# Moving layer-norm pieces and the order of GpSimd's work in a fused attention and FFN kernel

## The chip, the cores and the metric

The kernel runs on one core of one Trainium2 chip. The metric is the device time of one execution in microseconds (us). TensorE (PE in the profile) multiplies matrices, VectorE (DVE), ScalarE (ACT) and GpSimd (POOL) work on 128 partitions at once, and SyncE (SP) issues most of the DMA transfers. Each engine runs its own list of instructions in order and waits on semaphores for the others.

## What is computed

x has the shape 8 x 1024 x 128 (batch, position, channel). With H = 8 heads:

```python
def layer(x, proj_q, proj_k, proj_v, proj_o, w1, w2):
    xn = (x - mean(x)) / sqrt(var(x) + 1e-5)              # over the 128 channels
    Q = einsum('bnd,hdk->bhnk', xn, proj_q)
    K = einsum('bmd,dk->bmk', xn, proj_k)                 # one key head, one value head
    V = einsum('bmd,dv->bmv', xn, proj_v)
    weights = softmax(einsum('bhnk,bmk->bhnm', Q, K))
    O = einsum('bhnm,bmv->bhnv', weights, V)
    Y = einsum('bhnv,hdv->bnd', O, proj_o)
    mid = einsum('amh,ehn->aemn', xn, w1)                 # linear, 8 experts summed
    return x + Y + einsum('aemn,enh->amh', mid, w2)
```

## The kernel before

The weights are folded once at the start: query and key projections into one matrix per head (a_hi, a_lo), value and output projections into another (c_hi, c_lo), and the two FFN weights into a single 128 x 128 matrix (f_hi, f_lo). Every large product is done in float16 with operands split into a high half and a low half; the product of the two low halves is left out.

The 8192 positions are 64 tiles of 128. Work is cut into 64 pairs (batch, head), each of two blocks of 512 queries, each block of four units of 128 queries against all 1024 keys: 512 units, one for each period of the main loop. All engines count the same periods n, and nine more empty the pipeline. A pair is 8 periods; "period 3" below means n = 3 modulo 8.

In a period TensorE computes the high part of the scores of unit n (L499), turns the row of maxima of unit n-1 (L527), does one to three tiles of the products of weights with values of an older block (weigh, L398 to L400 on t_ps), some small products (small_products: the projection of the next block, head_out on s_ps, the FFN of one tile, the transposition of a normalised tile), then the low parts of the scores of unit n-1 (low_passes, L512 and L514), and at the end it transposes the key maxima of unit n (L523). The low passes of unit n-1 wait for the bias, which VectorE copies into a row of g_lo (place_bias, L742).

VectorE in period n: place_bias(n-1), the maximum over keys of unit n (max_of_keys, L729), then between_maxima(n) (scaling of head outputs L752/L756 and FFN outputs L764, the copy of a turned tile L769, the low half of the projection L725 or of the values t_lo L746), then find_max(n) (L734), then before_bias(n). In periods 3 and 7 (row_later) the maximum over keys is ahead of place_bias, and TensorE does both halves of the high pass in one piece. Tiles from number 10 (AHEAD) on are normalised one per pair, in before_bias: bn_stats (L805) in period 2, bn_aggr (L647) in period 3, plus EPS (L811) in period 6, and in the next pair the scaling `normalise` (L650) in period 2 and the cast to float16 `split_high` (L657) in period 3. GpSimd takes the power -1/2 (L317) in period 7 and the low half xn_low (L273) in period 4 of the next pair. Tile 10 + p belongs to pair p, so pairs 0 to 53 have one.

ScalarE: the exponentials of unit n-1 (L357), their high half p_high (L364), g_high (L351) in periods 1 and 5, t_high (L370) in periods 2 and 6. p_high is not done in periods 1 and 5 and twice in periods 2 and 6.

GpSimd: the low half p_low of unit n-1 (L281), the addition of head outputs to xacc (add_head, L293) and of FFN outputs (add_ffn, L299). Within a period the additions and the normalisation pieces stand ahead of p_low. weigh waits for all four low halves of its block.

exponentials(u) waits for p_low of unit u-4, since there are PR = 4 buffers of exponentials; scale_head(k, g) waits for the addition of block k-1 with the same g, since y_tmp has one buffer for each g.

## Time and profile before

| quantity | value |
| --- | --- |
| time, median of 3 runs | 1693.48 us (1692.24 to 1694.28) |
| time of the profiled execution | 1692.57 us |
| its span, first to last instruction | 1690.8 us |
| mean granted TensorE clock | 0.999 |
| busy: TensorE | 1655.1 us, 98% |
| busy: GpSimd | 1335.8 us, 79% |
| busy: ScalarE | 1294.1 us, 77% |
| busy: VectorE | 1281.2 us, 76% |
| weight loads | 1212.9 us, 72% |

The busy time of TensorE is modelled from starts, so 98% does not mean that it is at its peak; a short gap shows in the distance between the starts of two products, not always in the idle column. The granted clock is 1.00 at 2.4 GHz and 0.50 at 1.2 GHz.

### The profile page before, as it was taken

What the parts mean: (1) busy time and instruction counts of PE and PEld (TensorE: products, weight loads), DVE (VectorE), ACT (ScalarE), POOL (GpSimd) and SP (SyncE); (2) the same over time, 40 slices, a digit from 0 to 9 for tenths busy, and PEclk for the clock granted to TensorE, in tenths of its full rate; (3) what the DMA queues carried; (4) which work ended last, traced back from release to release, by engine and by line L of the source; (5) the groups of instructions that cost most, each with busy time, mean ns of one, the idle gap of its engine ahead of it and who ended that gap; (6) DMA issues with size and microseconds to landing.
All of it is one profiled execution on the core that took longest, in us unless ns stands there. A gap on an engine that the chain in (4) does not pass through costs nothing. (4 is left out here: it accounts for less than half of the span.)

```text
span 1690.8 us, 46211 instructions
## 1 busy us (share of the span) xinstructions
PE 1655.1 (98%) x18820; PEld 1212.9 (72%) x18820; DVE 1281.2 (76%) x2761; ACT 1294.1 (77%) x1296; POOL 1335.8 (79%) x956
## 2 busy tenths in 40 slices
PE   7999999999999999999999999999999999999997
PEld 6777777777777777777777777777777777777774
DVE  5777777777777777777777777777777777777774
ACT  4777777777777777777777777777777777877874
POOL 2687888788788788878878878887887888788785
PEclk9999999999999999999999999999999999999999
DMA  7000000000000000000000000000000000000000
GB/s 227 2 2 2 2 2 14 2 2 2 8 8 2 1 2 8 8 2 2 2 8 8 2 1 2 8 8 2 2 2 14 2 2 2 2 14 2 2 2 13
DMA packets 16175, 16.71 MB, mean 10 GB/s; under 512 B 416, under 2 KB 12192, under 8 KB 15968
## 3 DMA queue, kind: packets, MB, share of 16 engines
q1 hardware_dynamic: 14928, 13.24, 2.7%
q8 instruction: 152, 2.49, 0.6%
q10 hardware_dynamic: 1040, 0.52, 0.1%
q14 instruction: 55, 0.45, 0.1%
HBM read 9.57 MB, written 4.19 MB: 8 GB/s over the span
## 5 line engine op out<-in xcount | busy, mean ns | idle before, releaser
L281 POOL TENSOR_TENSOR pr_lo<-pr,pr_hi 128x1024 f16<-128x1024 f32 x512 | 1087.7, 2135 | 328.5 <-ACT pr_hi L364 328.5
L357 ACT ACTIVATE pr<-s_ps,boost,scale 128x1024 f32<-128x1024 f32 x512 | 616.9, 1205 | 241.3 <-PE s_ps L514 222.4
L729 DVE TENSOR_REDUCE key_max<-s_ps 128x128 f16<-128x1024 f32 x512 | 625.7, 1222 | 0.1
L364 ACT ACTIVATE pr_hi<-pr 128x1024 f16<-128x1024 f32 x512 | 525.4, 1051 | 8.1
L512 PE MATMUL s_ps<-g_lo,xT 128*128 128x128 f16 x4096 | 512.9, 219 | 2.1 <-DVE g_lo L742 1.0
L514 PE MATMUL s_ps<-g_hi,xT 128*128 128x128 f16 x4096 | 512.3, 219 | 0.0
L512 PEld LDWEIGHTS s_ps<-g_lo,xT 128*128 128x128 f16 x4096 | 399.3, 98 | 41.7 <-DVE g_lo L742 11.1
L514 PEld LDWEIGHTS s_ps<-g_hi,xT 128*128 128x128 f16 x4096 | 400.8, 98 | 29.9
L398 PE MATMUL t_ps<-pr_hi,xn_hi 128*128 128x512 f16 x1024 | 388.3, 379 | 16.9 <-POOL pr_lo L281 3.2
L400 PE MATMUL t_ps<-pr_hi,xn_lo 128*128 128x512 f16 x1024 | 388.4, 379 | 0.0
L399 PE MATMUL t_ps<-pr_lo,xn_hi 128*128 128x512 f16 x1024 | 388.4, 379 | 0.0
L499 PEld LDWEIGHTS s_ps<-g_hi,xT 128*128 128x128 f16 x4096 | 282.3, 98 | 91.7 <-ACT g_hi L351 1.4
L499 PE MATMUL s_ps<-g_hi,xT 128*128 128x128 f16 x4096 | 333.6, 219 | 1.9 <-ACT g_hi L351 1.2
L742 DVE CAST g_lo<-turn_ps 1x128 f16<-1x128 f32 x512 | 141.4, 276 | 177.0 <-PE turn_ps L527 172.4
L293 POOL TENSOR_TENSOR xacc<-xacc,y_tmp 128x256 f32<-128x256 f32 x256 | 186.6, 729 | 9.3 <-DVE y_tmp L756 9.1
L400 PEld LDWEIGHTS t_ps<-pr_hi,xn_lo 128*128 128x128 f16 x1024 | 100.0, 98 | 121.3 <-issue 0.6
L734 DVE TENSOR_REDUCE minus_max<-turn_ps 128x1 f16<-128x128 f16 x512 | 147.8, 289 | 39.2 <-PE turn_ps L523 38.9
L725 DVE TENSOR_TENSOR g_lo<-s_ps,g_hi 128x512 f16<-128x512 f32 x127 | 87.8, 691 | 90.0 <-ACT g_hi L351 90.0
L370 ACT ACTIVATE t_hi<-t_ps 128x512 f16<-128x512 f32 x128 | 76.4, 597 | 92.5 <-PE t_ps L400 92.5
L756 DVE SCALAR_TENSOR_TENSOR y_tmp<-s_ps,scale,recip 128x256 f32<-128x256 f32 x256 | 123.6, 483 | 26.9 <-DVE recip L752 0.5
L398 PEld LDWEIGHTS t_ps<-pr_hi,xn_hi 128*128 128x128 f16 x1024 | 99.9, 98 | 52.0 <-issue 31.9
L523 PE MATMUL turn_ps<-ident,key_max 128*128 128x128 f16 x512 | 112.1, 219 | 0.1
(117 smaller groups left out, 1548.0 us busy)
## 6 DMA issues: line engine op xcount, KB each, us to landing
out_dram<-xacc SPq DMA_DIRECT2D x16, 256.0 KB, 2.3
w_sb<-in_L_ffn_w_dram SPq DMA_DIRECT2D x1, 2048.0 KB, 10.0
pr<-in_L_attn_proj_q_dram ACTq DMA_DIRECT2D x1, 512.0 KB, 4.4
xacc<-in_L_attn_x_dram SPq DMA_DIRECT2D x2, 256.0 KB, 4.9
pr<-in_L_attn_proj_o_dram SPq DMA_DIRECT2D x1, 512.0 KB, 6.3
xacc<-in_L_attn_x_dram SPq DMA_DIRECT2D x1, 128.0 KB, 6.2
wkv<-in_L_attn_proj_k_dram SPq DMA_DIRECT2D x1, 64.0 KB, 2.7
wkv<-in_L_attn_proj_v_dram SPq DMA_DIRECT2D x1, 64.0 KB, 4.2
```

The lines of the kernel that those rows point to most:

```text
L281: pool.tensor_tensor(pr_lo[:, u % RING, :], pr32[:, u % PR, :], pr_hi[:, u % RING, :], ALU.subtract)\
L293: pool.tensor_tensor(acc, acc, y_tmp[:, g, :, :], ALU.add).then_inc(y_added, 1)
L357: act.activation(pr32[:, u % PR, :], both_banks(u), ACT.Exp, bias=boost[:, 0:1], scale=scale[:, 0:1])\
L364: act.activation(pr_hi[:, u % RING, :], pr32[:, u % PR, :], ACT.Copy).then_inc(p_hi_ready, 1)
L398: pe.matmul(dst, lhs_hi, rhs_hi, start=start, stop=False)
L399: pe.matmul(dst, lhs_hi, rhs_lo, start=False, stop=False)
L400: return pe.matmul(dst, lhs_lo, rhs_hi, start=False, stop=stop)
L499: last = pe.matmul(dst[:, i * P:(i + 1) * P], x_hi(keys + i), g_hi[:, k % 2, j * P:(j + 1) * P], start=i == 0, stop=False, skip_group_chec ...
L512: pe.matmul(dst, x_hi(batch_tile(k) + t), g_lo[:, k % 2, j * P:(j + 1) * P], start=False, stop=False, skip_group_check=True)
L514: last = pe.matmul(dst, x_lo(batch_tile(k) + t), g_hi[:, k % 2, j * P:(j + 1) * P], start=False, stop=True, skip_group_check=True)
L729: dve.tensor_reduce(key_max[:, u % 2, :], both_banks(u).rearrange("p (t q) -> p q t", q=P), AX_X, ALU.max).then_inc(keys_max, 1)
L734: dve.tensor_reduce(minus_max[:, u % 2, 0:1], turn16[:, 0:P], AX_X, ALU.max, negate=True)\
```

## The change

Seven edits. (1) In GpSimd's loop p_low(n-1) comes first in the period; the head additions that were in periods 3 modulo 4 and 0 modulo 4 come one period later, behind p_low. (2) VectorE's bn_stats, bn_aggr and plus EPS go from periods 2, 3 and 6 to 0, 1 and 4; the power goes from period 7 to 3. (3) The scaling `normalise` of tiles 10 and later goes from VectorE to GpSimd, in period 6 of the same pair (normalise_next). (4) Their cast split_high goes from VectorE to ScalarE, in period 0 of the next pair, behind p_high. (5) xn_low goes from period 4 to period 2 of the next pair. (6) In periods 0 and 4 TensorE does the FFN product and the transposition ahead of head_out(k-3, 1), and VectorE empties them in the same order. (7) The DMA of tiles 10 to 63 becomes two, of tiles 10 to 15 ahead of w2 and of 16 to 63 behind it. bn_aggr gets a wait for the scaling of the tile before (ln_xn32), since GpSimd reads the single slot of mean and variance.

```diff
--- before.py
+++ after.py
@@ -115,7 +115,7 @@
         turn16 = turn_ps[:, :].bitcast(F16)
 
         q_in, o_in, kv_in = sem("q_in"), sem("o_in"), sem("kv_in")
-        x_in = [sem("x_in%d" % n) for n in range(4)]
+        x_in = [sem("x_in%d" % n) for n in range(5)]
         w1_in, w2_in = sem("w1_in"), sem("w2_in")
         consts, slot_set = sem("consts"), sem("slot_set")
         transposed, evacuated, kv_ready, folded, c_copied = (
@@ -234,8 +234,9 @@
             sp.dma_start(wo_sb, wo.rearrange("h d v -> d h v")).then_inc(o_in, 16)
             sp.dma_start(xacc[:, NT:AHEAD, :], x_tiles[:, NT:AHEAD, :]).then_inc(x_in[2], 16)
             sp.dma_start(w1_sb[:, :, :], w1.rearrange("e h n -> h e n")).then_inc(w1_in, 16)
+            sp.dma_start(xacc[:, AHEAD:2 * NT, :], x_tiles[:, AHEAD:2 * NT, :]).then_inc(x_in[3], 16)
             sp.dma_start(w2_sb[:, :, :, :], w2.rearrange("e (c p) d -> p e c d", p=P)).then_inc(w2_in, 16)
-            sp.dma_start(xacc[:, AHEAD:TILES, :], x_tiles[:, AHEAD:TILES, :]).then_inc(x_in[3], 16)
+            sp.dma_start(xacc[:, 2 * NT:TILES, :], x_tiles[:, 2 * NT:TILES, :]).then_inc(x_in[4], 16)
 
             for b in range(B):
                 for half in range(2):
@@ -275,6 +276,14 @@
 
             xn_low(HT, HT, HT)
 
+            def normalise_next(tile):
+                pool.wait_ge(ln_rstd, tile + 1)
+
+                pool.wait_ge(ln_hi, tile)
+                pool.wait_ge(xn_ready, tile)
+                pool.tensor_scalar(xn32[:, 0, 1:D], xacc[:, tile, 1:D], mean_var[:, AHEAD, 0:1],
+                                   rstd[:, AHEAD:AHEAD + 1], ALU.subtract, ALU.mult).then_inc(ln_xn32, 1)
+
             def p_low(u):
 
                 pool.wait_ge(p_hi_ready, u + 1)
@@ -303,30 +312,36 @@
                 k, at = divmod(n, 4)
                 if n == 2:
                     xn_low(NT, NT, AHEAD - NT)
-                if at == 3 and 0 <= k - 2 < BLOCKS:
-                    add_head(k - 2, 0, ffn_adds)
-                    head_adds += 1
+                if 1 <= n <= UNITS:
+                    p_low(n - 1)
                 if at == 0 and 0 <= k - 3 < BLOCKS:
-                    add_head(k - 3, 1, ffn_adds)
+                    add_head(k - 3, 0, ffn_adds)
                     head_adds += 1
                 if (tile := ffn_tile(n)) is not None:
                     add_ffn(tile, head_adds)
                     ffn_adds += 1
-                if n % 8 == 7 and (tile := ln_tile(n // 8)) is not None:
+                if at == 1 and 0 <= k - 3 < BLOCKS:
+                    add_head(k - 3, 1, ffn_adds)
+                    head_adds += 1
+                if n % 8 == 3 and (tile := ln_tile(n // 8)) is not None:
                     pool.wait_ge(ln_var, tile - AHEAD + len(FIRST_TILES) + 1)
                     pool.tensor_tensor(rstd[:, AHEAD:AHEAD + 1], var_eps[:, AHEAD:AHEAD + 1],
                                        minus_half[:, 0:1], ALU.pow).then_inc(ln_rstd, 1)
-                if n % 8 == 4 and (tile := ln_tile(n // 8 - 1)) is not None:
+                if n % 8 == 6 and (tile := ln_tile(n // 8)) is not None:
+                    normalise_next(tile)
+                if n % 8 == 2 and (tile := ln_tile(n // 8 - 1)) is not None:
                     xn_low(tile, 0, 1)
-                if 1 <= n <= UNITS:
-                    p_low(n - 1)
 
         @block.scalar
         def _(act):
             act.dma_start(wq_sb, wq.rearrange("h d k -> d h k")).then_inc(q_in, 16)
-            def split_high(tile):
-                act.wait_ge(ln_xn32, tile + HT)
-                act.activation(xn_hi[:, tile:tile + HT, 1:D], xn32[:, tile:tile + HT, 1:D], ACT.Copy).then_inc(ln_hi, HT)
+            def split_high(tile, row, tiles):
+                act.wait_ge(ln_xn32, tile + tiles)
+                if tile > NT:
+                    act.wait_ge(ln_hi, tile)
+                at = tile % KEEP
+                act.activation(xn_hi[:, at:at + tiles, 1:D], xn32[:, row:row + tiles, 1:D], ACT.Copy)\
+                   .then_inc(ln_hi, tiles)
 
             def empty_w1(e):
                 act.wait_ge(w1_turned, e + 1)
@@ -334,10 +349,10 @@
 
             act.wait_ge(transposed, 2)
             act.activation(wqT, s_ps[:, 0:N].rearrange("p (h k) -> p h k", h=H), ACT.Copy).then_inc(evacuated, 1)
-            split_high(0)
+            split_high(0, 0, HT)
             act.wait_ge(transposed, 3)
             act.activation(woT, s_ps[:, N:2 * N], ACT.Copy).then_inc(evacuated, 1)
-            split_high(HT)
+            split_high(HT, HT, HT)
             act.wait_ge(folded, 2)
             act.activation(c32[:, :], s_ps[:, N:2 * N], ACT.Copy).then_inc(c_copied, 1)
             act.wait_ge(scales, 1)
@@ -387,6 +402,8 @@
                     p_high(n - 2)
                 if at != 1 and 1 <= n <= UNITS:
                     p_high(n - 1)
+                if n % 8 == 0 and (tile := ln_tile(n // 8 - 1)) is not None:
+                    split_high(tile, 0, 1)
                 if n == 7:
                     act.wait_ge(scales, 2)
                     act.activation(c_hi[:, :, 0:P], c32[:, :].rearrange("p (h k) -> p h k", h=H), ACT.Copy,
@@ -592,8 +609,6 @@
                     if k >= 3:
                         pe.wait_ge(y_scaled, 2 * (k - 2))
                     head_out(k - 2, 0)
-                if at == 0 and 0 <= k - 3 < BLOCKS:
-                    head_out(k - 3, 1)
                 if (tile := ffn_tile(n)) is not None:
                     pe.wait_ge(weights_ready, 4)
                     three_pass(ffn_part(n), x_hi(tile), x_lo(tile), f_hi[:, :], f_lo[:, :]).then_inc(ffn_ps, 1)
@@ -601,6 +616,8 @@
                     pe.wait_ge(xn_ready, tile + 1)
                     pe.transpose(turned_part(n)[:, 0:P], xn_hi[:, tile % KEEP, :], ident16[:, :])
                     pe.transpose(turned_part(n)[:, P:2 * P], xn_lo[:, tile % KEEP, :], ident16[:, :]).then_inc(xT_ps, 1)
+                if at == 0 and 0 <= k - 3 < BLOCKS:
+                    head_out(k - 3, 1)
 
             row_of_amax(0, None)
             turn_tiles(0)
@@ -772,12 +789,12 @@
             def between_maxima(n):
 
                 k, at = divmod(n, 4)
-                if at == 0 and 0 <= k - 3 < BLOCKS:
-                    scale_head(k - 3, 1)
                 if (tile := ffn_tile(n)) is not None:
                     scale_ffn(n, tile)
                 if (tile := turn_tile(n)) is not None:
                     copy_turned(n, tile)
+                if at == 0 and 0 <= k - 3 < BLOCKS:
+                    scale_head(k - 3, 1)
                 if at == 1 and k + 1 < BLOCKS:
                     g_low(k + 1)
                 if at == 2 and 0 <= k - 2 < BLOCKS:
@@ -799,22 +816,20 @@
             def before_bias(n):
 
                 pair, at = divmod(n, 8)
-                if at == 2 and (tile := ln_tile(pair)) is not None:
+                if at == 0 and (tile := ln_tile(pair)) is not None:
                     if pair == 0:
                         dve.wait_ge(x_in[3], 16)
+                    if tile == 2 * NT:
+                        dve.wait_ge(x_in[4], 16)
                     dve.bn_stats(stats[:, AHEAD, :], xacc[:, tile, :]).then_inc(ln_stats, 1)
-                if at == 3 and (tile := ln_tile(pair)) is not None:
+                if at == 1 and (tile := ln_tile(pair)) is not None:
                     dve.wait_ge(ln_stats, tile + 1)
+
+                    dve.wait_ge(ln_xn32, tile)
                     tile_mean(AHEAD)
-                if at == 6 and (tile := ln_tile(pair)) is not None:
+                if at == 4 and (tile := ln_tile(pair)) is not None:
                     dve.wait_ge(ln_mean, tile + 1)
                     dve.tensor_scalar_add(var_eps[:, AHEAD:AHEAD + 1], mean_var[:, AHEAD, 1:2], EPS).then_inc(ln_var, 1)
-                if at == 2 and (tile := ln_tile(pair - 1)) is not None:
-                    dve.wait_ge(ln_rstd, tile + 1)
-                    dve.wait_ge(xn_ready, tile)
-                    normalise(tile, AHEAD, 0)
-                if at == 3 and (tile := ln_tile(pair - 1)) is not None:
-                    split_high(tile, 0, 1)
                 if n == 0:
                     normalise_first(2)
                 if n == 1:
```

## Rows read from the trace of the kernel before

**Rows 1.** The page's first part: busy us (share) xinstructions of each engine.
```profile
PE 1655.1 (98%) x18820; PEld 1212.9 (72%) x18820; DVE 1281.2 (76%) x2761; ACT 1294.1 (77%) x1296; POOL 1335.8 (79%) x956
```
**Rows 2.** Waits: engine, line, waited for: us in total, times, longest us.
```profile
PEld t_ps L398 <- issue: 31.9, 126, 0.3
PEld s_ps L512 <- DVE g_lo L742: 11.1, 53, 1.0
```
**Rows 3.** Windows, key turn to key turn: us, busy of each engine, clock, DMA.
```profile
705.20:708.75 3.55, 3.42 (x41) 2.39 (x39) 3.24 (x8) 3.10 (x3) 1.15 (x2) 1.00 0.00 0
718.15:721.50 3.35, 3.24 (x41) 2.38 (x39) 2.79 (x7) 3.09 (x3) 1.08 (x2) 1.00 0.00 0
1423.12:1426.48 3.36, 3.25 (x42) 2.39 (x40) 2.99 (x7) 3.10 (x3) 0.96 (x2) 1.00 0.00 0
```
**Rows 4.** Timeline of DVE, period 3: start us, us, instruction, [idle before].
```profile
705.14 0.69 DVE L746 TENSOR_TENSOR t_lo<-t_ps,t_hi 128x512 f16<-128x512 f32 x1
705.94 0.28 DVE L805 BATCH_NORM_STATS2 stats<-xacc 128x6 f32<-128x128 f32 x1
706.14 0.33 DVE L650 TENSOR_SCALAR xn<-xacc,mean_var,rstd 128x127 f32<-128x127 f32 x1
707.52 0.27 DVE L742 CAST g_lo<-turn_ps 1x128 f16<-1x128 f32 x1
```
**Rows 5.** Timeline of DVE and PE around the turn of period 2.
```profile
703.00 0.28 DVE L734 TENSOR_REDUCE minus_max<-turn_ps 128x1 f16<-128x128 f16 x1
703.64 0.28 DVE L742 CAST g_lo<-turn_ps 1x128 f16<-1x128 f32 x1 [0.36 <-PE turn_ps L527]
...
703.38 0.22 PE L527 MATMUL turn_ps<-ident,minus_max 128*128 128x128 f16 x1
```
**Rows 6.** Timeline of ACT, periods 0, 1 and 3.
```profile
700.50 1.06 ACT L364 ACTIVATE pr_hi<-pr 128x1024 f16<-128x1024 f32 x1
701.76 0.60 ACT L351 ACTIVATE g_hi<-s_ps 128x512 f16<-128x512 f32 x1 [0.21 <-PE s_ps L400]
...
706.50 1.99 ACT L364 ACTIVATE pr_hi<-pr 128x1024 f16<-128x1024 f32 x2
```
**Rows 7.** Groups by line: shapes xcount | busy us, mean ns | idle before us.
```profile
L329 ACT ACTIVATE xn_hi<-xn 128x508 f16<-128x508 f32 x2 | 1.2, 618 | 0.0
L299 POOL TENSOR_TENSOR xacc<-xacc,ffn_tmp 128x128 f32<-128x128 f32 x64 | 29.1, 455 | 5.0
```
**Rows 8.** Timeline of POOL, period 7.
```profile
720.57 2.13 POOL L281 TENSOR_TENSOR pr_lo<-pr,pr_hi 128x1024 f16<-128x1024 f32 x1 [2.27 <-ACT pr_hi L364]
```
**Rows 9.** Timeline of DVE and PE in pair 1, period 4.
```profile
67.38 2.23 DVE L835 SCALAR_TENSOR_TENSOR f_lo<-f32w,inv_scale,f_hi 128x128 f16<-128x128 f32 x1
...
68.86 0.22 PE L400 MATMUL s_ps<-c_hi,t_lo 128*128 128x130 f16 x1
69.86 0.23 PE L512 MATMUL s_ps<-g_lo,xT 128*128 128x128 f16 x1 [0.78 <-DVE g_lo L742]
```
**Rows 10.** Line 657: duration ns min/median/max, first and last start us.
```profile
L657 DVE CAST xn_hi<-xn x55: 196/542/825, 31.5 to 1426.9; 128x127 f16<-128x127 f32 x54, 128x254 f16<-128x254 f32 x1
```
**Rows 11.** Timeline of POOL, the same stretch of pair 1.
```profile
65.24 4.22 POOL L281 TENSOR_TENSOR pr_lo<-pr,pr_hi 128x1024 f16<-128x1024 f32 x2 [3.58 <-ACT pr_hi L364]
```
**Rows 12.** The end: timelines of POOL and PE, and a window.
```profile
1673.05 0.72 POOL L293 TENSOR_TENSOR xacc<-xacc,y_tmp 128x256 f32<-128x256 f32 x1
...
1675.90 0.61 PE L398 MATMUL t_ps<-pr_hi,xn_hi 128*128 128x512 f16 x1 [3.25 <-POOL pr_lo L281]
...
1675.80:1679.20 3.40, 3.30 (x13) 1.65 (x14) 0.00 (x0) 0.00 (x0) 0.05 (x1) 0.50 0.00 0
```
**Rows 13.** The start: SP's timeline, DMA issue (us to landing), and PE.
```profile
7.92 10.72 SPq L238 DMA_DIRECT2D xacc<-in_L_attn_x_dram  x1
...
xacc<-in_L_attn_x_dram SPq DMA_DIRECT2D x1, 0.5 KB, 26.9
...
35.11 1.11 PE L551 MATMUL t_ps<-w_sb,w1T 128*128 128x128 f32 x8
```

## The prediction

> **What bounds the kernel now.** I read the busy line first: TensorE is at 98% of the span, the next engine, GpSimd, at 79% [rows 1]. So nothing is won by making another engine faster as such; only time that TensorE waits can go. The idle column hides most of such time, because the ends of products are modelled. The waits view names what is left of it, ahead of weight loads: 126 waits in front of the first tile of weigh, 31.9 us in all, and 53 waits of the low pass for the bias copy L742, 11.1 us [rows 2]. 53 is once a pair for the pairs that normalise a tile, except the first.
>
> The second wait is the one that the change touches. To size it, compare key turn to key turn for periods that hold the same products: period 3 of pair 26 lasts 3.55 us, period 7 of the same pair 3.35, and period 3 of pair 54, the first that has no bn_stats any more, 3.36 [rows 3]. The VectorE column shows why: 3.24 us busy with 8 instructions in the first, 2.79 with 7 in the second. In the timeline of period 3, t_lo is followed (behind find_max) by bn_stats, 0.28, and normalise, 0.33, ahead of the key maximum, and only then comes the bias copy, done at 707.52 + 0.27 = 707.79 [rows 4]. In this period the key maximum is ahead of the bias copy, so two small instructions push the low pass directly. Pair 54 still has the normalise and no bn_stats, and does not stall: one of the two fits, both do not.
>
> The first wait stays. TensorE comes to weigh when t_lo is not done: it starts at 705.14 and takes 0.69 [rows 4]. Its chain (last product of the old block, ScalarE's t_hi, t_lo) contains nothing that is moved, and periods 3 and 7 both have it.
>
> **The change part by part.**
>
> *Periods 0, 1, 4 for the statistics, normalise and cast off VectorE.* Period 3 gets back the difference: 3.55 - 3.36 = 0.19 to 3.55 - 3.35 = 0.20, taken as 0.195. Pairs 2 to 53 are 52, so 52 x 0.195 = 10.1 us. bn_stats now lies between find_max(0) and the bias copy of period 1, and bn_aggr between find_max(1) and the copy of period 2, where VectorE sits idle 0.36 us before the copy [rows 5]. bn_aggr is shorter than bn_stats at 0.28, so it fits, and the copy keeps its time because it waits for TensorE's row. Cost nothing; without that cover it would be up to 0.28 a pair, 15 us. Both ends of the new waits on VectorE (ln_xn32 for the tile before) are most of a pair old.
>
> *The cast on ScalarE.* Its price comes from its two nearest rows: 1.06 us for 1024 elements [rows 6] and 0.618 for 508 [rows 7], 0.86 ns an element, so 0.618 - 381 x 0.00086 = 0.29 us for 127, say 0.30; the upper end is 0.62, the lower zero. It stands behind p_high of period 0, which ends at 700.50 + 1.06 = 701.56, and ahead of g_high, which starts at 701.76 with 0.21 idle before it, waiting for the projection [rows 6]. The cast ends at 701.86, or 701.76 if it overlaps the instruction before it by the 0.1 us by which the two p_high of period 3 do (1.99 us for both, against twice 1.06) [rows 6]. A later g_high is not free: g_low and find_max stand behind it on VectorE. find_max(1) ends at 703.00 + 0.28 = 703.28 and TensorE's row of maxima starts at 703.38 [rows 5]. I take the 0.10 between them as the passing of the semaphore, so that there is no room. Then every delay of g_high counts in full, 54 times. I take no delay, since g_high can itself overlap the cast's end; the range keeps 0 to 0.1 us, 0 to 5.4 us in all.
>
> *GpSimd.* It gets one scaling of 127 elements a pair. The trace has no such instruction on GpSimd; nearest is an addition of two 128 x 128 operands, 455 ns [rows 7]. With two operations in it I put its bounds at 0.2 and 0.91 and take 0.46. GpSimd does not set the pace: it waits 2.27 us for p_high before p_low of unit 4 at 720.57 [rows 8]. From there in the new order: p_low 2.13, one head addition 0.72, p_low 2.13, scaling 0.46, so the scaled tile is ready at about 726.0. A pair lasts 25.64, since 28 of them lie between 705.20 and 1423.12 [rows 3], so the cast's place is 701.46 + 25.64 = 727.1. Room 1.1 us. The moved addition has a reader too: VectorE may not write y_tmp again before it is done. It ends at 720.57 + 2.13 + 0.72 = 723.4, and VectorE writes that buffer in the period that begins with the key turn at 721.50, behind a bias copy, a whole key maximum and a reciprocal; I take it as in time, and if it is not, VectorE waits one for one. The power waits for plus EPS of period 4, but GpSimd reaches that point one period of p_low later. The weights' low halves come earlier than now, never later.
>
> *The stretch where the FFN weights are split.* In pair 1 the subtraction f_lo, 128 x 128, took 2.23 us [rows 9]. It started at 67.38, just after GpSimd's second p_low began at 65.24 + 2.11 = 67.35, and ended with it at 69.46 [rows 11]. TensorE's low pass started 1.00 us after the last product of head_out, 0.78 of it idle, so 0.78 to 1.00 was lost [rows 9]. After the change the cast (196 ns at best [rows 10]) and bn_aggr ahead of it are gone, so f_lo comes 0.2 us sooner, while GpSimd's first p_low still runs. The steady casts L657 meet a running p_low of 2.13 us and take 542 ns in the median [rows 8, 10]: they get in at the boundary between two. f_lo should do the same. Gain 0.9 us, with bounds 1.0 and 0, where it meets the start of a p_low again. The Trainium skill has the rule, "SBUF — State Buffer", Who interferes with whom: VectorE with two SBUF inputs or in a two-port mode and GpSimd lock each other out for a whole instruction, and who issues first wins. By that rule f_lo loses the whole of a p_low again if it comes second, and nothing if it comes first; the trace agrees with the lock itself (196 against 542 ns).
>
> *The order of GpSimd at the end.* The last weigh waits 3.25 us for the last p_low, at 1675.90, and between that and the p_low before stands an addition of 0.72 [rows 12]. The one before the last but one p_low also leaves, but one comes in two places earlier; one net goes. With an overlap of 0.04 the gain is 0.7 us. Behind this wait TensorE ran at 0.50 of its clock (1.2 GHz) for 3.40 us [rows 12], which costs about half of that, 1.7 us. With the idle stretch cut to 2.55 us it may or may not fall again; I count nothing and keep 1.7 us for the lower end.
>
> *The DMA split.* The last input transfer, issued at 7.92, landed 26.9 us later, 34.8, and w2 is first used at 35.11 [rows 13]. The bytes are the same and w2 still is not last, so it lands before 34.8. VectorE asks for tile 10 two periods sooner than before, but its part of the transfer has lost w2 and 48 of 54 tiles from in front of it. Nothing; a wait there would come once.
>
> *The order of FFN, transposition and head_out in periods 0 and 4.* The same products and the same VectorE work in another order. head_out's sums come two or three products later, while VectorE still empties the FFN or the turned tile, and the group is ended by a find_max that waits for the key turn. Nothing; from above it is bounded by one product's 0.22 us [rows 9] in each of these periods, from below by nothing gained, since no wait stands there.
>
> **Sum.** 10.1 + 0.9 + 0.7 = 11.7 us. The profiled execution took 1692.57 for a span of 1690.8, so 1680.9 on its terms. The median of the runs is 0.9 higher, 1693.48, which gives 1681.8.
>
> **The rivals.**
>
> *A, the cast delays g_high.* For: zero room in the chain behind it, and a price between 0.30 and 0.62. Against: 0.21 idle plus an overlap of 0.1. With g_high 0.1 late, 1681.8 + 5.4 = 1687.2. Chance 0.17.
>
> *B, GpSimd becomes the pace, slower than before.* If the scaling takes long, the cast waits for it on ScalarE, with g_high, the exponentials and all of VectorE's chain behind. Room is 1.1 us, so it begins at 0.46 + 1.1 = 1.6 us for one scaling, and it eats the gain from 1.8 us on (0.2 us in 54 pairs). Were it as dear as a p_low, 2.13, the delay is 0.5 x 54 = 28 us: 1681.8 + 28 = 1710. For: no row has this form on GpSimd. Against: the addition of its size takes 0.46, and a scaling reads one operand less. Chance 0.05. The Trainium skill, "GPSIMD Engine Reference", Engine selection, speaks against this part of the change: elementwise work belongs on VectorE. Against it, here VectorE's instruction is what TensorE waits for, and GpSimd has the idle time [rows 8].
>
> *C, the stall only moves.* bn_stats or bn_aggr push the copies of periods 1 and 2, and the 0.19 us come back there. For: VectorE's chain around period 2 is tight. Against: 0.36 idle against at most 0.28. Time 1681.8 + 10 = 1692, the same as before. Chance 0.06.
>
> **How the numbers follow.** Forecast 0.72, A 0.17, C 0.06, B 0.05. The predicted time is the forecast's, 1681.8. The lower end takes in the clock, 1681.8 - 1.7 - 0.9 for the spread of the runs (1692.24 to 1694.28) = 1679.2; the upper end is A's, 1687.2. Beyond it lie B and C, 0.11. A measurement of this kernel can tell about 0.2%, 3.4 us: A and the forecast are faster, C the same, B slower, hence 0.89, 0.06, 0.05.
>
> **What would show it.** Right: period 3 lasts 3.35 as period 7; the 53 waits on L742 are gone and the 126 of weigh remain with about 32 us; pairs last 25.64 - 0.195 = 25.45; f_lo under 0.6 us; the last wait for p_low about 2.55. Wrong: a new wait of TensorE for find_max L734 or for the bias copy in periods 1 and 2 (A, C), ScalarE's cast waiting for GpSimd's scaling (B), or a pair still at 25.64.

## The result, and the profile after

The changed kernel takes 1679.36 us in the median (1679.04 to 1680.03) against 1693.88 for the kernel before on the same chip: 0.9917 of it, with an interval of [0.9899, 0.9934]. Forecast were 1681.8 us and a range of 1679.2 to 1687.2, so the median lies 0.16 us above the lower end of the range. The profiled execution took 1679.06 us for a span of 1677.3, so 13.5 us of span went.

The page's busy line of the changed kernel, and then two rows of its waits (engine, line, waited for: us, times, longest), which answer to [rows 1, 2]:

```profile
PE 1644.3 (98%) x18820; PEld 1212.4 (72%) x18820; DVE 1241.3 (74%) x2653; ACT 1304.8 (78%) x1350; POOL 1381.8 (82%) x1010
```

```profile
PEld t_ps L415 <- issue: 31.7, 125, 0.3
...
PE t_ps L415 <- POOL pr_lo L290: 2.6, 1, 2.6
```

108 instructions left VectorE (54 normalise, 54 casts), 54 each came to ScalarE and GpSimd. The wait ahead of weigh is as it was, 31.7 us in 125 places; by the distance between the starts of two products it costs 0.27 us each time. The 53 waits of the low pass for the bias copy are gone: of its rows one is left, 0.2 us, once.

Windows of the changed kernel from key turn to key turn (us, busy of PE, PEld, DVE, ACT, POOL, clock, DMA): period 2, period 3, period 7 of a steady pair, then the whole pair.

```profile
696.65:699.40 2.75, 2.75 (x35) 2.04 (x33) 2.43 (x6) 1.80 (x2) 2.75 (x3) 1.00 0.01 3
699.40:702.76 3.36, 3.25 (x42) 2.39 (x40) 2.74 (x6) 3.10 (x3) 1.27 (x2) 1.00 0.00 0
712.15:715.51 3.36, 3.25 (x42) 2.40 (x39) 2.73 (x6) 3.10 (x3) 1.75 (x3) 1.00 0.02 5
...
690.06:715.51 25.45, 25.23 (x295) 18.56 (x292) 19.21 (x42) 20.24 (x21) 21.75 (x17) 1.00 0.01 2
```

Period 3 lasts as long as period 7, where it was 0.2 us longer before [rows 3]. VectorE has 6 instructions in it instead of 8, and in its timeline (start us, us, instruction) nothing stands between find_max and the key maximum, as bn_stats and normalise did [rows 4]:

```profile
699.34 0.69 DVE L763 TENSOR_TENSOR t_lo<-t_ps,t_hi 128x512 f16<-128x512 f32 x1
699.95 0.28 DVE L751 TENSOR_REDUCE minus_max<-turn_ps 128x1 f16<-128x128 f16 x1
700.14 1.21 DVE L746 TENSOR_REDUCE key_max<-s_ps 128x128 f16<-128x1024 f32 x1
701.28 0.27 DVE L759 CAST g_lo<-turn_ps 1x128 f16<-1x128 f32 x1
```

To see where the 13.5 us went, I cut the span at key turns. "Stretch" below is the time between two of them:

| stretch | before | after | gained |
|---|---|---|---|
| start to key turn 15 (pairs 0 and 1) | 80.50 | 79.36 | 1.14 |
| pairs 2 to 63, up to key turn 511 | 1586.52 | 1576.42 | 10.1 |
| from there to the end | 23.77 | 21.50 | 2.27 |

The first row is 1.18 us in the period of f_lo (4.27 to 3.09) and 0.07 in the one before it, less 0.13 of a later start. The middle row is 52 times 0.195, for the pairs that still have statistics to make: such a pair lasts 25.446 instead of 25.641.

### The profile page after: what moved, and what is told of

It reads as the page before. It is cut to its first block and busy times, and to the rows that moved or that the text cites. A ratio compares the mean times of both kernels' runs of the same rounds, so it can differ in the third digit from the quotient of the medians.

```text
span 1677.3 us, 46384 instructions
## 1 busy us (share of the span) xinstructions
PE 1644.3 (98%) x18820; PEld 1212.4 (72%) x18820; DVE 1241.3 (74%) x2653; ACT 1304.8 (78%) x1350; POOL 1381.8 (82%) x1010
## 5 line engine op out<-in xcount | busy, mean ns | idle before, releaser
L415 PEld LDWEIGHTS t_ps<-pr_hi,xn_hi 128*128 128x128 f16 x1024 | 99.8, 97 | 51.2 <-issue 31.7
```

Of the source, the lines that this page charges most:

```text
L415: pe.matmul(dst, lhs_hi, rhs_hi, start=start, stop=False)
```

## The experiments

Each code cut shows the lines that carry the edit; `...` stands for lines left out.

**Is it the place of the statistics?** On the kernel before, bn_stats and bn_aggr alone go two periods later. All else, the normalise and the cast on VectorE among it, stays.

```
-                if at == 2 and (tile := ln_tile(pair)) is not None:
+                if at == 4 and (tile := ln_tile(pair)) is not None:
...
-                if at == 3 and (tile := ln_tile(pair)) is not None:
+                if at == 5 and (tile := ln_tile(pair)) is not None:
```

> The kernel before, with bn_stats moved from period 2 to 4 and bn_aggr from 3 to 5, nothing else. Theory (VectorE's two instructions ahead of the key maximum of period 3 make the stall, and one alone fits): all of the steady gain comes, period 3 lasts 3.35 to 3.36 us in pairs 2 to 53, a pair 25.45, time 10.1 us less, 1683.5. The stretch of f_lo and the end stay as before. Rival 1 (the gain comes from GpSimd's order, or from its and ScalarE's taking over the work): 1693.5, a pair 25.64. Rival 2 (both moved and offloaded needed): between, above 1686.

Measured: 1683.64 us, 0.9942 [0.9927, 0.9957]. Period 3 of its trace, same columns as above:

```profile
701.74:705.10 3.36, 3.25 (x42) 2.39 (x40) 2.99 (x7) 3.10 (x3) 0.96 (x2) 1.00 0.00 0
```

It has 7 VectorE instructions, as pair 54 had before, and the same 3.36. The pair lasts 25.447, to 0.001 us what the whole change gives. So one of the two small instructions was enough to take away, and moving the statistics alone gives all that the change gains in the steady pairs. The change takes the other one, normalise, off VectorE as well; whether that alone would have done the same was not tried.

**Or is it GpSimd's order?** On the kernel before, p_low goes to the head of its turn, and the two head additions go behind it and one period later, as in the change. Nothing else is changed.

```
-                if at == 3 and 0 <= k - 2 < BLOCKS:
-                    add_head(k - 2, 0, ffn_adds)
-                    head_adds += 1
+                if 1 <= n <= UNITS:
+                    p_low(n - 1)
                 if at == 0 and 0 <= k - 3 < BLOCKS:
-                    add_head(k - 3, 1, ffn_adds)
+                    add_head(k - 3, 0, ffn_adds)
...
+                if at == 1 and 0 <= k - 3 < BLOCKS:
+                    add_head(k - 3, 1, ffn_adds)
+                    head_adds += 1
...
-                if 1 <= n <= UNITS:
-                    p_low(n - 1)
```

> The kernel before, with GpSimd's p_low first in the period and the head additions one period later, nothing else. Theory: a pair stays at 25.64 us, the 53 waits for the bias copy stay; only the end changes, where the last wait for p_low goes from 3.25 to about 2.57 us (0.7 us), and with it, if the clock does not fall to 0.50 before the last products of weigh, another 1.6: 1691.2 to 1692.8. Rival (GpSimd's order made the gain): 1683 or less.

Measured: 1693.91 us in the median of ten runs (1692.03 to 1694.46), 1.0002 [0.9993, 1.0012], pairs of 25.641 and a period 3 of 3.551. The order gives nothing in the steady pairs. It does shorten the last wait for p_low to 2.6 us, from 3.25 [rows 12]:

```profile
PE t_ps L398 <- POOL pr_lo L281: 2.6, 1, 2.6
```

The time from the last key turn to the end falls by 0.81 us, and yet the time is the same. The loss is in pair 1, where the projection weights are split. The period from key turn 8 to 9 lasts 5.20 us instead of 3.81, which is 1.39 us lost. These are the rows of VectorE's subtraction c_lo: before, then with the new order alone, then in the change. The last has GpSimd's instruction of that moment beside it:

```profile
56.30 1.28 DVE L830 SCALAR_TENSOR_TENSOR c_lo<-c,inv_scale,c_hi 128x1024 f16<-128x1024 f32 x1 [0.16 <-ACT c_hi L392]
```

```profile
56.67 3.10 DVE L830 SCALAR_TENSOR_TENSOR c_lo<-c,inv_scale,c_hi 128x1024 f16<-128x1024 f32 x1 [0.16 <-ACT c_hi L392]
```

```profile
56.43 1.28 DVE L845 SCALAR_TENSOR_TENSOR c_lo<-c,inv_scale,c_hi 128x1024 f16<-128x1024 f32 x1
...
56.35 1.90 POOL L284 TENSOR_SCALAR xn<-xacc,mean_var,rstd 128x127 f32<-128x127 f32 x1
```

With the order alone c_lo waits out a p_low. In the whole change the small scaling stands there on GpSimd, and now GpSimd waits for VectorE (1.90 us for a scaling that takes 0.83 elsewhere); in the kernel before it was the power, 0.55 us at 56.19. The later experiments fit this: in those that keep the scaling on GpSimd c_lo takes 1.28 to 1.46 us, in the two that put it back on VectorE 2.97 and 2.96. So this order needs the scaling on GpSimd beside it; alone it costs more (1.39) than it gives (0.81). The prediction did not see this, since it looked for such collisions at f_lo and not at c_lo.

**The price of the stall from the other side.** On the changed kernel the statistics go back to periods 2 and 3, and a scaling into an unread buffer stands behind bn_stats, in the place of the old normalise.

```
-                if at == 0 and (tile := ln_tile(pair)) is not None:
+                if at == 2 and (tile := ln_tile(pair)) is not None:
...
+                    dve.tensor_scalar(spare[:, 1:D], xacc[:, tile, 1:D], mean_var[:, 0, 0:1], rstd[:, 0:1],
+                                      ALU.subtract, ALU.mult)
-                if at == 1 and (tile := ln_tile(pair)) is not None:
+                if at == 3 and (tile := ln_tile(pair)) is not None:
```

> The changed kernel, with bn_stats and bn_aggr back in periods 2 and 3 and, behind bn_stats, one scaling of 127 elements on VectorE whose output nobody reads, so that VectorE again has two instructions ahead of the key maximum of period 3, while GpSimd and ScalarE keep their new work and order. Theory: the stall returns in full, 53 or 54 times 0.195 = 10.4 us, period 3 at 3.55: 1689.8. Rival (the gain came from the other engines): 1679.4 to 1681.

Measured: 1689.17 us in the median of ten runs (seven at 1688.7 to 1690.0, three at 1691.8 to 1692.0), 0.9979 [0.997, 0.9988], which is 9.8 us above the change. Its periods 3 and 7:

```profile
703.88:707.42 3.54, 3.41 (x41) 2.38 (x39) 3.24 (x8) 3.10 (x3) 1.45 (x2) 1.00 0.00 0
...
716.82:720.17 3.35, 3.24 (x41) 2.39 (x39) 2.73 (x6) 3.10 (x3) 1.54 (x3) 1.00 0.02 5
```

Eight instructions and 3.24 us of VectorE bring back the long period, with everything else of the change in place: pairs 2 to 63 take 1586.52 us together, exactly as before the change. Together with the first experiment this settles the large term from both sides.

**How much room has g_high?** On the changed kernel ScalarE makes the cast twice, the second time into a spare buffer.

```
                     split_high(tile, 0, 1)
+                    act.activation(spare[:, 1:D], xn32[:, 0, 1:D], ACT.Copy)
```

> The changed kernel, with ScalarE's cast of the normalised tile done twice (the second into a spare tile). It measures the price of rival A: the chain from g_high over g_low and find_max to the row of maxima has no room. Theory: in the changed kernel g_high starts 0.007 us after the cast and still in its old place, so a second cast of 0.29 less 0.10 overlap delays it by 0.19 to 0.20 us in each of 54 pairs, all of it lost: 10.3 to 10.8 us more, 1690. Rival (there is room behind g_high): 1679.4 to 1682.

Measured: 1682.29 us, 0.9938 [0.9922, 0.9955]. ScalarE's timeline of the changed kernel, then of this one, and last the window of this one's period 2:

```profile
694.70 1.06 ACT L379 ACTIVATE pr_hi<-pr 128x1024 f16<-128x1024 f32 x1
695.66 0.29 ACT L343 ACTIVATE xn_hi<-xn 128x127 f16<-128x127 f32 x1
695.96 0.60 ACT L366 ACTIVATE g_hi<-s_ps 128x512 f16<-128x512 f32 x1
```

```profile
696.48 0.29 ACT L344 ACTIVATE xn_hi<-xn 128x127 f16<-128x127 f32 x1
696.68 0.29 ACT L408 ACTIVATE spare<-xn 128x127 f16<-128x127 f32 x1
696.88 0.58 ACT L367 ACTIVATE g_hi<-s_ps 128x512 f16<-128x512 f32 x1
```

```profile
697.47:700.26 2.79, 2.79 (x35) 2.04 (x33) 2.48 (x6) 1.80 (x2) 2.79 (x3) 1.00 0.01 3
```

In the change the cast starts 0.10 us before p_high ends and g_high starts when the cast's row ends, which is where TensorE's product let it start before [rows 6]. A second cast takes 0.29 us but starts 0.20 after the first, and g_high starts 0.20 after it, since neighbours overlap. In the change g_high started 0.30 after the cast, so it moves by only 0.1 us and not by the 0.19 to 0.20 that were expected, which counted one overlap and not two. Period 2 grows from 2.747 to 2.792, 0.045 us, 54 times 2.4 us; the medians are 2.9 apart, with runs of this kernel from 1680.95 to 1684.28. Rival A was a real danger, but half as dear as it was put.

**How much room has GpSimd?** One and two more scalings ahead of the real one, into spare buffers. The edit shown is that with two; with one the range is shorter.

```
+                for i in range(2):
+                    pool.tensor_scalar(spare[:, i, 1:D], xacc[:, tile, 1:D], mean_var[:, AHEAD, 0:1],
+                                       rstd[:, AHEAD:AHEAD + 1], ALU.subtract, ALU.mult)
```

> The changed kernel, with GpSimd's scaling of a tile done twice (the first into a spare tile). It measures the room of rival B. In the changed kernel a scaling takes 0.83 us, ends at 4.80 us after the key turn that opens the pair, and ScalarE's cast starts at 5.60, so the room is 0.80. Theory: a second scaling just uses it up: 0 to 2 us more than the changed kernel, 1679.4 to 1681.5. Rival (GpSimd, at 82%, already sets the pace somewhere): 54 x 0.8 = 43 us more, 1722.

> The changed kernel, with GpSimd's scaling done three times (two into spare tiles): 1.66 us more a pair against a room of 0.80. Theory: the cast waits for the last scaling, about 0.85 us late, g_high 0.75 late, and all but 0.03 of it is lost in each of 54 pairs: 39 us more, 1718, slower than the kernel before. Rival (there is more room, since low halves can run up to four units behind): under 1690.

Measured: with one more 1679.92 us, 0.9922 [0.9907, 0.9937], and pairs of 25.444: nothing. With two more 1717.96 us, 1.0146 [1.013, 1.0161], and pairs of 26.135. What one scaling takes in the changed kernel (group by line: xcount | busy us, mean ns | idle), and the waits with three:

```profile
L284 POOL TENSOR_SCALAR xn<-xacc,mean_var,rstd 128x127 f32<-128x127 f32 x54 | 45.8, 849 | 0.0
```

```profile
PEld turn_ps L548 <- DVE minus_max L755: 36.7, 54, 0.7
...
ACT xn_hi L347 <- POOL xn L288: 39.6, 54, 0.8
```

This is rival B, brought about on purpose: ScalarE's cast waits 0.73 us for GpSimd in every pair, and TensorE's turn of the maxima waits for all that stands behind it, 54 times 0.68. The threshold lies between one and two extra scalings. With two, 2 x 0.83 = 1.66 us are added and 0.69 arrive in the pair (less than the 0.73 that the cast waits, as g_high has its little room), so the room beside the real one is some 0.9.

**The order of FFN, transposition and head_out.** On the changed kernel the second half of head_out and its scaling go back ahead of FFN and transposition.

```
+                if at == 0 and 0 <= k - 3 < BLOCKS:
+                    head_out(k - 3, 1)
                 if (tile := ffn_tile(n)) is not None:
...
-                if at == 0 and 0 <= k - 3 < BLOCKS:
-                    head_out(k - 3, 1)
...
```

> The changed kernel, with the order of the kernel before in periods 0 and 4: head_out(k-3, 1) ahead of the FFN product and the transposition, and VectorE's emptying likewise. Theory: nothing, 1679.0 to 1680.0, periods 0 and 4 as long as in the changed kernel. Rival (this order carries part of the gain): 1682 or more.

Measured: 1679.56 us, 0.9921 [0.9904, 0.9937], all periods the same to 0.001 us. This part does nothing to the time.

**Why f_lo got short.** On the kernel before, f_lo goes from the end of its turn to its head, ahead of normalise and cast.

```
             def before_bias(n):
+                if n == 11:
+                    dve.wait_ge(hi_ready, 3)
+                    dve.scalar_tensor_tensor(out=f_lo[:, :], in0=f32w[:, :], scalar=inv_scale[:, 2:3], in1=f_hi[:, :],
+                                             op0=ALU.mult, op1=ALU.subtract).then_inc(weights_ready, 1)
...
```

> The kernel before, with f_lo of period 11 ahead of bn_aggr and the cast instead of behind them, nothing else. Theory (f_lo lost 1.2 us only because it came just after GpSimd had begun a p_low): it starts 0.2 us sooner, gets in at the boundary, takes 0.3 to 0.5 us instead of 2.23, and the stretch from key turn 11 to key turn 12 falls from 4.27 us to 3.1 to 3.3; everything else as before, 1692.5. Rival (it waits for a whole p_low wherever it stands): 4.3 us.

Measured: 1693.76 us in a single run, beside 1693.44 for the kernel before. Its VectorE and GpSimd timelines, then those of the changed kernel:

```profile
68.02 0.34 DVE L804 SCALAR_TENSOR_TENSOR f_lo<-f32w,inv_scale,f_hi 128x128 f16<-128x128 f32 x1
68.37 2.07 DVE L657 CAST xn_hi<-xn 128x127 f16<-128x127 f32 x1
```

```profile
66.07 4.29 POOL L281 TENSOR_TENSOR pr_lo<-pr,pr_hi 128x1024 f16<-128x1024 f32 x2 [3.58 <-ACT pr_hi L364]
```

```profile
67.24 0.41 DVE L850 SCALAR_TENSOR_TENSOR f_lo<-f32w,inv_scale,f_hi 128x128 f16<-128x128 f32 x1
```

```profile
65.37 4.27 POOL L290 TENSOR_TENSOR pr_lo<-pr,pr_hi 128x1024 f16<-128x1024 f32 x2 [2.94 <-ACT pr_hi L379]
```

f_lo is short, but the cast, which follows it behind bn_aggr, takes 2.07 us and ends at 70.44, about when the second p_low does. The period takes 4.26 us (4.27 before), not the 3.1 to 3.3 that were expected. So the collision is not a property of f_lo: here VectorE gets f_lo in at the boundary between two p_low, and the cast meets the p_low that has begun. In the changed kernel the cast is no longer on VectorE, f_lo is alone there, and the period takes 3.09. The Trainium skill, "SBUF — State Buffer", Who interferes with whom, has a cast among the instructions that can take the shared port pair, and says that the order of issue decides who waits for a whole instruction; this trace agrees, with 2.07 us for the cast that started after the second p_low had begun, at 68.20.

**What the other wait is worth.** The 125 waits ahead of weigh are untouched by the change. On the changed kernel ScalarE first copies t out of its bank in fp32 and makes t_hi from the copy, weigh waits for the copy only, and GpSimd makes t_lo.

```
+                act.activation(t32[:, :], t_ps[:, :], ACT.Copy).then_inc(t_copied, 1)
+                act.wait_ge(t_copied, k + 1)
...
-                act.activation(t_hi[:, :], t_ps[:, :], ACT.Copy).then_inc(t_hi_ready, 1)
+                act.activation(t_hi[:, :], t32[:, :], ACT.Copy).then_inc(t_hi_ready, 1)
...
-                        pe.wait_ge(t_lo_ready, k)
+                        pe.wait_ge(t_copied, k)
...
+                    pool.tensor_tensor(t_lo[:, :], t32[:, :], t_hi[:, :], ALU.subtract).then_inc(t_lo_ready, 1)
```

> The changed kernel, with the other wait taken away, the one of the first tile of weigh for t_lo: ScalarE first copies the bank t_ps to SBUF in float32 (0.60 us), which frees the bank for the next block, then makes the high half from the copy, and GpSimd makes the low half from the copy in the place where it waits for p_high. VectorE loses its 0.69 us. Theory (the 126 waits of 0.27 us are the only loss left in a steady period, and TensorE is otherwise at its own pace): 2 x 0.272 us a pair, some 33 to 34 us less, a pair 24.90, 1646. Rival 1: the exponentials, 0.3 us later in periods 2 and 6, become the bound, and half or more of it stays: 1660 to 1680. Rival 2: GpSimd, with 128 x 1.2 us more, makes head_out wait: above 1660.

Measured: 1662.06 us, 0.9814 [0.9799, 0.9828]: 17.3 us under the change, half of the 33 expected. Its periods 3 and 7, and GpSimd's timeline in the second:

```profile
691.68:694.82 3.14, 3.14 (x43) 2.32 (x40) 2.30 (x5) 3.14 (x4) 2.26 (x3) 1.00 0.00 0
...
704.21:707.50 3.29, 3.24 (x41) 2.31 (x39) 2.29 (x5) 3.29 (x4) 2.98 (x5) 1.00 0.02 5
```

```profile
704.32 0.73 POOL L304 TENSOR_TENSOR xacc<-xacc,y_tmp 128x256 f32<-128x256 f32 x1
705.01 1.17 POOL L324 TENSOR_TENSOR t_lo<-t,t_hi 128x512 f16<-128x512 f32 x1
```

Period 3 falls by 0.22 us and period 7 by 0.07 only: t_lo, 1.17 us on GpSimd where VectorE took 0.69, comes behind a head addition there, and head_out has to wait for it. That is the second rival of the expectation. Beside the 3.09 us that both periods take in the last kernel below, this costs 0.05 us in period 3 and 0.20 in period 7. A pair lasts 25.159. From the first key turn to the last the gain over the change is 20.3 us; 3.5 are given back at the end. Part of that is the clock, which in this execution fell at the last weigh:

```profile
1645.50:1648.90 3.40, 3.15 (x14) 1.46 (x13) 0.65 (x2) 0.00 (x0) 1.92 (x3) 0.51 0.02 5
```

**Can the scaling go back to VectorE then?** VectorE has room without t_lo. On the last kernel, normalise goes back there at period 0 of the next pair, and the power and the low part of the tile are moved to fit.

```
+                if at == 0 and (tile := ln_tile(pair - 1)) is not None:
+                    dve.wait_ge(ln_rstd, tile + 1)
...
+                    normalise(tile, AHEAD, 0)
```

> The kernel with the early release of t_ps, and GpSimd relieved ahead of the t_lo of periods 7: the power in period 5, the scaling on VectorE in period 0 of the next pair (VectorE has lost t_lo and stands idle there 0.63 us), xn_low in period 0. In the kernel with the early release head_out waits 0.18 us in period 7 and 0.054 in period 3 for t_lo on GpSimd. Theory (GpSimd was late in period 7 by its own queue): the 0.18 goes to 0.054 as in period 3, a pair 25.03 instead of 25.16, 8 us less, 1654. Rival (it is something else): 1660 to 1662.

Measured: 1657.56 us, 0.9789 [0.9774, 0.9804]; pairs of 25.044, periods 3 and 7 at 3.13. The expectation was 1654. Period 1 grew from 3.394 to 3.435, and this is why:

```profile
710.52 1.39 DVE L666 TENSOR_SCALAR xn<-xacc,mean_var,rstd 128x127 f32<-128x127 f32 x1
```

Next to a running p_low the scaling takes 1.39 us, not the 0.33 of [rows 4]. c_lo takes 2.97 us, nearly as in the kernel with the new order alone, and its period 5.72 instead of 3.81. These two, 2.2 and 1.9 us, are about what is missing from the expectation.

**Halves.** t_hi and t_lo are made in two halves of 256 columns, and the two groups of head_out wait for one half each; first on the kernel just shown, then with the scaling on GpSimd.

```
+                    for i, half in enumerate((slice(0, 256), slice(256, 512))):
+                        pool.wait_ge(t_hi_ready, 2 * (k - 2) + i + 1)
+                        pool.tensor_tensor(t_lo[:, half], t32[:, half], t_hi[:, half], ALU.subtract)\
+                            .then_inc(t_lo_ready, 1)
```

> As the one before, with t_high and t_lo done in two halves of 256 columns, so that GpSimd starts 0.23 us sooner and the first head_out needs only the first half. Theory: no wait of head_out is left, a pair 24.90, 6.5 us less than that kernel, 1648. Rival (the exponentials, another 0.08 us later, become the bound; or the two more dispatches on GpSimd cost what the halves give): 1654 or more.

Measured: 1659.63 us, 0.98 [0.9783, 0.9816], 2.1 us above the kernel before it where 6.5 less were expected. Periods 3 and 7 fall to 3.087, yet period 1 grows to 3.571. The scaling on VectorE stands longer in p_low, 1.53 us in the median against 1.40, and these 0.14 us are what period 1 grew by (durations in ns, min/median/max, first of the kernel before it, then of this one):

```profile
L666 DVE TENSOR_SCALAR xn<-xacc,mean_var,rstd x64: 332/1397/1416, 9.5 to 1386.7; 128x127 f32<-128x127 f32 x64
...
L670 DVE TENSOR_SCALAR xn<-xacc,mean_var,rstd x64: 333/1533/1547, 9.8 to 1389.3; 128x127 f32<-128x127 f32 x64
```

For the last one, from the kernel with the early release: halves, the scaling kept on GpSimd in period 6, the power in period 4 and the low part of the tile in period 0.

```
-                if n % 8 == 3 and (tile := ln_tile(n // 8)) is not None:
+                if n % 8 == 4 and (tile := ln_tile(n // 8)) is not None:
...
-                if n % 8 == 2 and (tile := ln_tile(n // 8 - 1)) is not None:
+                if n % 8 == 0 and (tile := ln_tile(n // 8 - 1)) is not None:
```

> The kernel with the early release of t_ps, halves of t_high and t_lo as in the one before, but the scaling stays on GpSimd in period 6, since on VectorE in period 0 it stood 1.4 to 1.5 us in the lock of a running p_low; the power goes to period 4 and xn_low to period 0, into GpSimd's idle stretches. Theory: head_out does not wait (as with the halves before), the key maximum of period 1 is on time again, c_lo of period 8 meets the short scaling and not a p_low; a pair 24.91, which is TensorE's own pace with no wait left, against 25.16 in the first early release: 15 us less than its 1662, 1646 to 1648. Rival (GpSimd at 92% is the bound in some period now): 1652 or more.

Measured: 1646.55 us (1646.15 to 1647.31), 0.9724 [0.9708, 0.974]: the fastest of all, 32.8 us under the change. Its busy line, a period 3 and a pair:

```profile
PE 1625.3 (99%) x18820; PEld 1205.3 (73%) x18820; DVE 1177.6 (72%) x2525; ACT 1369.4 (83%) x1606; POOL 1542.1 (94%) x1266
```

```profile
686.40:689.49 3.09, 3.09 (x41) 2.34 (x39) 2.29 (x5) 3.09 (x5) 2.91 (x6) 1.00 0.00 0
...
677.07:701.97 24.90, 24.90 (x294) 18.44 (x292) 18.19 (x40) 21.23 (x26) 24.25 (x21) 1.00 0.04 13
```

TensorE is busy 24.90 of 24.90 us. Since busy time is modelled, the starts say it better. These are the last seven high products of a period 3 (the start of the first of them) and the first product of weigh behind them, in the change and then in this kernel:

```profile
699.51 0.55 PE L516 MATMUL s_ps<-g_hi,xT 128*128 128x128 f16 x7
700.18 0.38 PE L415 MATMUL t_ps<-pr_hi,xn_hi 128*128 128x512 f16 x1
```

```profile
686.52 0.55 PE L528 MATMUL s_ps<-g_hi,xT 128*128 128x128 f16 x7
686.91 0.38 PE L427 MATMUL t_ps<-pr_hi,xn_hi 128*128 128x512 f16 x1
```

From the first start to the second there are 0.67 us in the change and 0.39 here. In the whole pair 26 of this kernel every product starts 0.06 us (128 columns) or 0.22 us (512) after the one before it, so in the steady pairs no stall is left. Against the change a pair is 0.54 us shorter, 0.27 in each of periods 3 and 7; the mean of the wait column was near it, 0.25 us (31.7 by 125). To make the halves straight out of the bank without the fp32 copy, VectorE on the first while ScalarE reads the second, wasn't tried.

## Why the prediction was right, point by point

- **What bounds the kernel, and the period that was long.** Right in kind and size: 10.1 us predicted, 10.1 measured over the steady pairs, and one instruction of the two is enough, as pair 54 had shown [rows 3]. The new pair of 25.45 was predicted as well.
- **The wait of weigh stays.** Right, 31.7 us. The last kernel shows that it was real time and not an artefact of the modelled ends.
- **The statistics fit in periods 1 and 2 (rival C).** Right. The two periods last 3.394 and 2.747 us as before the change. Before the bias copies of those periods VectorE is still idle, 0.43 and 0.27 us, and bn_aggr takes 0.17:

```profile
694.44 0.28 DVE L759 CAST g_lo<-turn_ps 1x128 f16<-1x128 f32 x1 [0.43 <-PE turn_ps L544]
...
697.40 0.17 DVE L664 BATCH_NORM_AGGREGATE mean_var<-stats 128x2 f32<-128x6 f32 x1
...
697.84 0.28 DVE L759 CAST g_lo<-turn_ps 1x128 f16<-1x128 f32 x1 [0.27 <-PE turn_ps L544]
```

- **The cast (rival A).** Price right, 0.29 us, and g_high begins as early as it can. That there is "no room" behind it was wrong by a little: a g_high 0.1 us late cost 0.045 a pair and not 0.1, so A's end of the range, 5.4 us, was twice too dear for that delay. Some of the 0.10 us that were put down to the semaphore was slack; which part, only this difference says.
- **GpSimd's scaling (rival B).** This term was mis-sized. Taken was 0.46 us from the addition next to it; it is 0.83 to 0.85, nearly the upper bound. The place for it was about the size forecast: the point from which it decides was put at 1.6 us for one scaling, and 1.67 us (two of them) cost nothing, while 2.5 (three) cost 0.69 a pair, which puts the point near 1.8. So the scaling comes free, but with 0.9 us left and not 1.1. The sentence from the Trainium skill, "GPSIMD Engine Reference", Engine selection, that elementwise work belongs on VectorE, names a true price (0.83 against 0.33 us) that here lay beside TensorE's work, up to that point.
- **f_lo.** 0.9 us predicted, 1.18 measured in its period and 0.07 in the one before. The lost time was taken from TensorE's idle column, 0.78 to 1.00; the difference of the two periods would have been the better measure. The reason stated, 0.2 us sooner, holds only half: f_lo alone made sooner was short and gained nothing, since the cast stood behind it.
- **GpSimd's order at the end.** 0.7 us predicted; the wait fell from 3.25 to 2.57, 0.68. The 1.7 us for the clock were left out of the forecast and kept for the lower end of the range, and most of them came: this is the last weigh (PE with its idle time, and a window):

```profile
1663.98 0.39 PE L415 MATMUL t_ps<-pr_hi,xn_hi 128*128 128x512 f16 x1 [2.57 <-POOL pr_lo L290]
```

```profile
1663.90:1667.30 3.40, 3.32 (x25) 1.90 (x26) 0.65 (x2) 0.00 (x0) 1.98 (x4) 1.00 0.02 5
```

At 1.00 the same 3.40 us hold 25 products where they held 13 at 0.50 [rows 12]. The end gained 2.27, and the new order alone, where the clock fell as before, gained 0.81 there, so 1.5 us are the clock. That this execution kept the clock is partly luck. In the profiled execution with one more scaling the same wait was 2.56 us long, the clock fell, and from the last key turn to the end it took 23.01 us instead of 21.50:

```profile
1665.29 0.61 PE L419 MATMUL t_ps<-pr_hi,xn_hi 128*128 128x512 f16 x1 [2.56 <-POOL pr_lo L294]
...
1665.20:1668.60 3.40, 3.31 (x13) 1.62 (x14) 0.00 (x0) 0.00 (x0) 1.44 (x3) 0.53 0.02 5
```

The 2.4 us by which the median lies under the forecast are then 1.6 more at the end than forecast, 0.2 more in the stretch with f_lo, and 0.6 because the median lies only 0.3 above the profiled execution, where the forecast took 0.9.
- **The DMA split and the order of products.** Nothing, as predicted; for the products the experiment shows it, for the split only that no wait for it appeared.
- **Not foreseen:** the 1.4 us that GpSimd's new order costs at c_lo when it comes alone. The change escapes it by the small scaling that it puts in that place, which the prediction did not reckon with, so that the sum was right there by luck.

## What to carry to other kernels

Size a stall by comparing two periods that hold the same products, one with and one without the suspected instruction; that gave 10.1 us to a decimal, where sums of idle columns did not. An instruction that fits in an engine's total time can still cost its length if it stands between a result and the chain that feeds the busiest engine, so move small work to where the engine waits anyway, and look at each place where the moved work can make another engine's instruction wait for a whole one of its own. When the busiest engine waits for a buffer to be emptied in two steps, one plain copy that frees it first can be worth more than reordering: here 17.3 us by itself and 32.8 with the halves and two small moves after it, against 14.5 for the change.

## What the runs showed of the hardware

- **A scaling on GpSimd is dear for its size.** With 127 elements and two per-partition operands it took 0.83 us alone and 1.90 beside c_lo, against 0.455 for an addition of two operands of 128 [rows 7]. On VectorE it was 0.33 alone and 1.39 beside p_low.
- **An instruction of VectorE can be held for the rest of one of GpSimd's.** c_lo took 1.28 or 3.10 us, f_lo 0.41 or 2.23, a cast 0.20 [rows 10] or 2.07, and a small edit elsewhere decided which.
- **The length of the idle time alone does not decide whether the clock falls.** Six profiled kernels with the scaling on GpSimd have a last wait for p_low of 2.56 to 2.57 us. After it the clock stayed at 1.00 (2.4 GHz) in the change, with the two instructions back, with the cast done twice and with the old order of products, and it fell towards 0.50 (1.2 GHz; 0.53 and 0.52 over 3.4 us) with one and with two more scalings. After 2.57 us it fell with the new order alone. After 2.94 us it fell in the kernel with the early release, but not in the last one, whose window is:

```profile
1631.16:1634.56 3.40, 3.40 (x25) 1.88 (x26) 0.66 (x2) 0.00 (x0) 3.17 (x5) 1.00 0.02 5
```

What does decide stays open: these are single executions, and no kernel was made to vary it.
